# Attention with clipped Q, K, V on one core: the attention stage's queues rearranged, normalising moved from VectorE to GpSimd

## The reference

```python
xn = _layernorm(x, axis=-1)
# attention, 32 heads of 32 features
qkv = jnp.clip(jnp.einsum('bsd,ed->bse', xn, Wqkv), -8.0, 8.0)
q, k, v = jnp.split(qkv, 3, axis=-1)
q = _layer_norm(q, q_ln_w, q_ln_b); k = _layer_norm(k, k_ln_w, k_ln_b)
scores = jnp.einsum('bqhd,bkhd->bhqk', q, k) * scale + slopes * rel   # causal mask
out = jnp.einsum('bhqk,bkhd->bqhd', softmax(scores), v)
x = x + jnp.einsum('bsd,ed->bse', out, Wout) + ffn(xn, W_binarized, bias)
```

## Time and profile before

| | us |
|---|---|
| median of 3 runs | 1588.84 (1585.44 to 1590.82) |
| the profiled execution | 1590.43, span 1588.6 |
| attention, first exponential to first output product | 727.4 to 1416.7 |
| output stage, from there to the end | 1416.7 to 1588.6 |

### The profile page before, as it was taken

How to read it: one execution, slowest core, us unless ns; L and a number is a source line. 1 busy time by engine, 2 the same in 40 slices (tenths; PEclk the granted TensorE clock), 3 DMA queues, 4 the chain that set the end, 5 groups by cost and what they waited for, 6 DMA issues and landing times.

```text
span 1588.6 us, 24448 instructions
## 1 busy us (share of the span) xinstructions
PE 1430.5 (90%) x9256; PEld 661.4 (42%) x9256; DVE 835.1 (53%) x1310; ACT 558.9 (35%) x1049; POOL 549.5 (35%) x316
## 2 busy tenths in 40 slices
PE   4899999999999979998888888887978888889998
PEld 2455445445545434444333333333333333334443
DVE  6665354545454301266767677666666677631111
ACT  4444133323333200004554555454554555540000
POOL 4221122222222100001544555543345555565443
PEclk9999999999999989999999999999999999999999
DMA  6453232322222372211222222212222220025543
GB/s 232 154 166 112 67 78 60 79 60 69 70 73 66 90 204 80 77 57 42 69 69 64 67 69 56 52 46 63 70 69 64 67 69 24 20 82 166 159 146 119
DMA packets 145396, 136.85 MB, mean 86 GB/s; under 512 B 83744, under 2 KB 112416, under 8 KB 145120
## 3 DMA queue, kind: packets, MB, share of 16 engines
q1 hardware_dynamic: 48285, 90.80, 18.4%
q10 hardware_dynamic: 97027, 44.89, 12.0%
HBM read 93.06 MB, written 42.47 MB: 85 GB/s over the span
## 4 chain that ended last, share of the span: by engine, by line
PE 64%; issue 10%; DVE 10%; ACT 4%; DMA 4%; ACTq 3%; POOL 3%; SPq 2%; POOLq 0%; DVEq 0%
PE ps L956 39%; PE ps L1115 8%; PE ps L1031 5%; DVE arena L836 5%; PE ps L1092 5%; DVE arena L892 3%; ACT arena L672 3%; PE ps L1118 3%; PE ps L1009 2%; PE ps L1095 1%; PE ps L1034 1%; ACTq L335 1%; DMA arena<-r_scr 1%; ACTq L336 1%; DMA v_scr<-arena 1%
## 5 line engine op out<-in xcount | busy, mean ns | idle before, releaser
L956 PE MATMUL ps<-arena 128*128 128x512 f16 x3584 | 795.5, 382 | 21.6 <-DVE arena L807 11.3
L956 PEld LDWEIGHTS ps<-arena 128*128 128x128 f16 (+1 forms) x3584 | 349.8, 98 | 439.3 <-issue 13.7
L556 POOL TENSOR_TENSOR arena<-arena 128x2048 f32<-128x2048 f32 (+1 forms) x96 | 338.4, 3525 | 551.3 <-ACT arena L672 542.0
L836 DVE TENSOR_REDUCE arena<-ps 128x1 f16<-128x512 f32 (+3 forms) x768 | 382.3, 548 | 213.9 <-PE ps L1034 121.1
L672 ACT ACTIVATE arena<-ps 128x512 f32<-128x512 f32 (+3 forms) x768 | 326.9, 499 | 294.8 <-PE ps L1095 182.8
L1031 PE MATMUL ps<-arena 127*128 127x512 f16 (+3 forms) x768 | 249.4, 346 | 57.9 <-DVE arena L836 55.7
L1092 PE MATMUL ps<-arena 128*128 128x512 f16 (+3 forms) x768 | 253.0, 343 | 49.4 <-ACT arena L672 46.7
L807 DVE TENSOR_SCALAR arena<-ps 128x1024 f32<-128x1024 f32 x48 | 58.8, 1224 | 253.8 <-PE ps L956 225.0
L1115 PE MATMUL ps<-arena 128*32 128x512 f32 (+3 forms) x1536 | 163.4, 522 | 0.0
L1092 PEld LDWEIGHTS ps<-arena 128*128 128x128 f16 x768 | 77.0, 101 | 169.0 <-ACT arena L672 75.6
L1031 PEld LDWEIGHTS ps<-arena 127*128 127x128 f16 x768 | 76.9, 101 | 135.9 <-DVE arena L836 99.6
(11 more groups left out here) (50 smaller groups left out, 843.5 us busy)
## 6 DMA issues: line engine op xcount, KB each, us to landing
arena<-in_x SPq DMA_DIRECT2D x32, 512.0 KB, 4.6
arena<-in_wqkv_t SPq DMA_DIRECT2D x48, 256.0 KB, 4.0
base_scr<-arena SPq DMA_DIRECT2D x16, 512.0 KB, 2.9
q_scr<-arena ACTq DMA_DIRECT2D x16, 512.0 KB, 4.1
k_scr<-arena ACTq DMA_DIRECT2D x16, 512.0 KB, 4.4
v_scr<-arena SPq DMA_DIRECT2D x16, 512.0 KB, 2.9
arena<-r_scr SPq DMA_DIRECT2D x128, 64.0 KB, 2.0
arena<-base_scr SPq DMA_DIRECT2D x16, 512.0 KB, 3.8
```

The lines of the kernel that those rows point to most:

```text
L556: nc.gpsimd.tensor_tensor(acc[:, :, at:HALF], before, p32[k % PSLOTS][:, :, 0:w], ALU.add)\
L836: ins = nc.vector.tensor_reduce(negm[s % 2][:, at:at + 1], ps[:, NATB[use(s, pos) % RB], col:col + width], AX, ALU.max, negate=True)
L956: ins = nc.tensor.matmul(dst[c], lhs(k, a), wparts[:, k, b, c * HALF:(c + 1) * HALF], start=(k == 0 and (a, b) == order[0]), stop=(k == KT ...
```

## The change

The work is the same; its places change.

- The natural-score items of the next group are spread over the chunks by a table, `NATS`, and the V products get places by a table, `PV_AFTER`.
- `load_stack` and `load_vg` move from ACT's queue to SP's, behind the sums of the former group, two groups ahead in place of three.
- `o_norm` and `o_low` move from DVE to GpSimd, between the additions; in the output stage they stand ahead of the residual additions.
- O and S are copied with two ACT instructions, each with a semaphore of its own; `o_high` of the first half stands behind the exponential (0, 3) of the next group, that of the second half behind (8, 1).
- ACT and DVE no longer wait for the storing of V before attention starts; the first writers of `ot` do.

```diff
@@ -286,9 +287,17 @@
             at = max(0, P * t - HALF * qb)
             return qb, t, at, HALF - at
 
-        WORK = [span(c)[3] for c in range(NC) for j in range(GH)]
-        DUE = [ITEMS * sum(WORK[:x + 1]) // sum(WORK) for x in range(len(WORK))]
-        LAG = 2
+        NATS = [4, 3, 3, 2, 5, 4, 4, 4, 5, 4, 2, 2]
+        assert sum(NATS) == ITEMS
+
+        PV_AFTER = {(1, 0): [-2], (2, 0): [-1], (2, 3): [0], (4, 2): [1], (5, 2): [2], (6, 2): [3],
+                    (7, 1): [4], (8, 1): [5], (8, 3): [6], (10, 0): [7, 8], (11, 2): [9]}
+
+        def due(c, j):
+
+            return sum(NATS[:c]) + NATS[c] * (j + 1) // GH
+
 
 
         DIRECT = [qb == 0 or t == 0 for qb, t in CHUNKS]
@@ -413,7 +422,7 @@
 
             def sums_out(m):
 
-                sp.wait_ge(os_out, m + 1)
+                sp.wait_ge(s_out, m + 1)
                 sp.dma_start(s_scr[m], os_sb[m % 2][0:P:DH, 1, :]).then_inc(s_st, 16)
                 sp.wait_ge(s_st, 16 * (m + 1))
                 need(sp, rec_done, m - 1)
@@ -466,6 +475,14 @@
                 row_b_in(n)
                 if n > 0:
                     sums_out(blk_no(n - 1, 1))
+                    if n == 1:
+                        for s in range(2):
+                            sp.wait_ge(v_st[s], stored(NT // 2))
+                    if n < GROUPS - 1:
+                        load_vg(sp, n + 1)
+                    if n + 2 < GROUPS:
+                        sp.wait_ge(st_done, NC * GH * n)
+                        load_stack(sp, n + 2)
                 if n < GROUPS - 1:
                     row_a_in(n + 1)
                 if n > 0:
@@ -542,19 +559,51 @@
                 tile_loop(pool, qk_step)
 
 
+            def o_norm(n, qb):
+
+                m = blk_no(n, qb)
+                pool.wait_ge(r_ld, 16 * GH * (m + 1))
+                o = os_sb[m % 2][:, 0, :]
+                nc.gpsimd.tensor_tensor(o, o, rb[m % 2], ALU.mult).then_inc(on_done, 1)
+
+            def o_low(n, qb):
+
+                m = blk_no(n, qb)
+                pool.wait_ge(oh_done, m + 1)
+                if (n, qb) == (0, 0):
+                    for s in range(2):
+                        pool.wait_ge(v_st[s], stored(NT // 2))
+                part = [ot[n][:, s, qb * HALF:(qb + 1) * HALF] for s in range(2)]
+                nc.gpsimd.tensor_tensor(part[1], os_sb[m % 2][:, 0, :], part[0], ALU.subtract).then_inc(ol_done, 1)
+
+            def add_in(n, c):
+
+                qb, t, at, w = span(c)
+                k = n * NC + c
+                pool.wait_ge(exp_done, GH * (k + 1))
+                if t == 2:
+                    need(pool, pv_done, n * NC)
+                need(pool, add_done, adds_for(k) - 1)
+                former = p32[(k - 1) % PSLOTS] if t == 2 else acc[:, :, at:HALF]
+                nc.gpsimd.tensor_tensor(acc[:, :, at:HALF], former, p32[k % PSLOTS][:, :, 0:w], ALU.add)\
+                  .then_inc(add_done, 1)
+
             for n in range(GROUPS):
                 for c in range(NC):
-                    qb, t, at, w = span(c)
-                    k = n * NC + c
-                    if DIRECT[c] or t == 1:
-                        continue
-                    pool.wait_ge(exp_done, GH * (k + 1))
-                    if t == 2:
-                        need(pool, pv_done, n * NC)
-                    need(pool, add_done, adds_for(k) - 1)
-                    before = p32[(k - 1) % PSLOTS] if t == 2 else acc[:, :, at:HALF]
-                    nc.gpsimd.tensor_tensor(acc[:, :, at:HALF], before, p32[k % PSLOTS][:, :, 0:w], ALU.add)\
-                      .then_inc(add_done, 1)
+                    if not DIRECT[c] and CHUNKS[c][1] > 1:
+                        add_in(n, c)
+                    if n > 0:
+                        if c == 0:
+                            o_norm(n - 1, 0)
+                        if c == 2:
+                            o_low(n - 1, 0)
+                        if c == 6:
+                            o_norm(n - 1, 1)
+                        if c == 9:
+                            o_low(n - 1, 1)
+            for qb in range(2):
+                o_norm(GROUPS - 1, qb)
+                o_low(GROUPS - 1, qb)
 
             pool.wait_ge(bias_ld, 16)
             for t in range(NT):
@@ -677,34 +726,35 @@
                 m = blk_no(n, qb)
                 act.wait_ge(pv_done, n * NC + QB_END[qb] + 1)
                 need(act, ol_done, m - 1)
-                nc.scalar.activation(os_sb[m % 2], ps[:, O_BANK:O_BANK + 2, :], ACT.Copy).then_inc(os_out, 1)
+                nc.scalar.activation(os_sb[m % 2][:, 0, :], ps[:, O_BANK, :], ACT.Copy).then_inc(o_out, 1)
+                nc.scalar.activation(os_sb[m % 2][:, 1, :], ps[:, S_BANK, :], ACT.Copy).then_inc(s_out, 1)
 
             def o_high(n, qb):
 
                 m = blk_no(n, qb)
                 act.wait_ge(on_done, m + 1)
+                if (n, qb) == (0, 0):
+                    for s in range(2):
+                        act.wait_ge(v_st[s], stored(NT // 2))
                 nc.scalar.activation(ot[n][:, 0, qb * HALF:(qb + 1) * HALF], os_sb[m % 2][:, 0, :], ACT.Copy)\
                   .then_inc(oh_done, 1)
 
             act.wait_ge(mm_done, NT * 4)
             act.wait_ge(w_lo, ready(NT * 4 - 1))
-            for s in range(2):
-                act.wait_ge(v_st[s], stored(NT // 2))
             for n in range(GROUPS):
                 for c in range(NC):
                     for j in range(GH):
                         exps(n, c, j)
-                        if (c, j) == (2, 1) and n > 0:
-                            os_copy(n - 1, 1)
-                            if n < GROUPS - 1:
-                                load_vg(act, n + 1)
-                        if (c, j) == (7, 1) and n > 0:
-                            o_high(n - 1, 1)
-                        if (c, j) == (6, 1):
+                        if n > 0:
+                            if (c, j) == (0, 3):
+                                o_high(n - 1, 0)
+                            if (c, j) == (2, 0):
+                                os_copy(n - 1, 1)
+                            if (c, j) == (8, 1):
+                                o_high(n - 1, 1)
+                        if (c, j) == (6, 2):
                             os_copy(n, 0)
-                if n < GROUPS - STACKS:
-                    load_stack(act, n + STACKS)
-                o_high(n, 0)
+            o_high(GROUPS - 1, 0)
             os_copy(GROUPS - 1, 1)
             o_high(GROUPS - 1, 1)
 
@@ -877,40 +927,16 @@
                 need(dve, r_st, 16 * (m - 1))
                 nc.vector.reciprocal(rout[m % 2], rin[m % 2]).then_inc(rec_done, 1)
 
-            def o_norm(n, qb):
-
-                m = blk_no(n, qb)
-                dve.wait_ge(r_ld, 16 * GH * (m + 1))
-                o = os_sb[m % 2][:, 0, :]
-                nc.vector.tensor_tensor(o, o, rb[m % 2], ALU.mult).then_inc(on_done, 1)
-
-            def o_low(n, qb):
-
-                m = blk_no(n, qb)
-                dve.wait_ge(oh_done, m + 1)
-                part = [ot[n][:, s, qb * HALF:(qb + 1) * HALF] for s in range(2)]
-                nc.vector.tensor_tensor(part[1], os_sb[m % 2][:, 0, :], part[0], ALU.subtract).then_inc(ol_done, 1)
-
-            dve.wait_ge(v_st[1], stored(NT // 2))
             for n in range(GROUPS):
                 for pos in range(ITEMS):
                     if n < GROUPS - 1:
                         nat_item(n + 1, pos)
                     elif pos == 0:
                         row_out(n, use(GROUPS, 0), row_b, rowb_ld)
-                    if n > 0:
-                        if pos == 4:
-                            o_low(n - 1, 0)
-                        if pos == 16:
-                            recips(n - 1, 1)
-                        if pos == 23:
-                            o_norm(n - 1, 1)
-                        if pos == 30:
-                            o_low(n - 1, 1)
+                    if pos == 16 and n > 0:
+                        recips(n - 1, 1)
                     if pos == 31:
                         recips(n, 0)
-                    if pos == 38:
-                        o_norm(n, 0)
 
             def c_out_step(t, p):
                 dve.wait_ge(c_done, t + 1)
@@ -919,11 +945,8 @@
                 nc.vector.scalar_tensor_tensor(outc[p], banks(4 + 2 * p, 2), 1.0 / (SX * SW), basec[p],
                                                ALU.mult, ALU.add).then_inc(c_out, 1)
 
-            o_low(GROUPS - 1, 0)
+            recips(GROUPS - 1, 1)
             c_out_step(0, 0)
-            recips(GROUPS - 1, 1)
-            o_norm(GROUPS - 1, 1)
-            o_low(GROUPS - 1, 1)
             for t in range(1, NT):
                 c_out_step(t, t % 2)
 
...
@@ -1104,7 +1127,7 @@
                 p, v = p32[k % PSLOTS], vg[n % 2]
                 pe.wait_ge(exp_done, GH * (k + 1))
                 if first:
-                    need(pe, os_out, blk_no(n, qb))
+                    need(pe, o_out, blk_no(n, qb))
```

(19 more changed lines are left out.)

## The result

The changed kernel took 1596.61 us in the median of 8 runs (1594.12 to 1600.18), the kernel before 1589.44 (8 runs beside them): a ratio of 1.005, 95% interval 1.0035 to 1.0065. It is slower by half a per cent, 7 us, where 26 had been forecast. The profiled execution has a span of 1593.8 us against 1588.6, 5.2 more.

What follows compares the result with a forecast made beforehand. GpSimd's queue, through ScalarE's wait for o_norm, was taken to bound the changed kernel's groups. Groups +18.0, head -3.3, tail +11 gave +25.7 on 1590.43, 1616.1; that execution is 1.6 above the median, so 1615, range 1580 to 1645.

Steps and rivals of the forecast that it cites:

- The bound that it named: Attention groups: GpSimd's queue ends last; ScalarE waits 8 us for o_norm at o_high, TensorE some 7.
- The tail: Output stage: o_norm and o_low ahead of tile 0's additions stop TensorE 8.6 us before product 2; with slow clock +11.
- The loads: Eight loads on SP's queue ahead of the reciprocals: counted at nothing, with cover of 1 us only.
- The larger stops of before: TensorE's stops of 3.36 us for VectorE and 3.00 for ScalarE: removing them buys nothing in the groups.
- S: Rest of a group's ring, from exponential (1', 0) to the next first addition: 19.3 us, bounds 16.6 and 21.
- the slow clock: TensorE at half speed behind its stop of 7 us in each group: 1.8 us, taken into 19.3.
- All groups: Attention, first addition of group 0 to group 15: 385.6 + 15 S = 675.1 us against 657.1, +18.0.
- GpSimd's chain: Each group, first addition to exponential (1', 0): 26.0 us with o_high and handovers, of which six additions 21.15.
- a sign: Trace after the change: the group's period would be 45 to 46 us.
- The head: Before attention: ScalarE's first exponential no longer waits for the storing of V, worth -3.3 us.

Runs made afterwards that it cites:

- e2: Changed kernel with ScalarE's o_high of the first half behind exponential (3, 3) of the next group instead of (0, 3); 1548.1 us, ratio 0.974.
- e1: Changed kernel with GpSimd's o_norm and o_low of the very last half behind the residual additions of tiles 0 and 1, c_out earlier; 1588.3 us.
- e12: Changed kernel with the loads on SP's queue issued at the end of a group, behind the reciprocals of both halves; 1597.0 us, ratio 1.0038.
- e7: Changed kernel with o_norm and o_low back on VectorE and the output stage's additions ahead as before the change; 1556.4 us, ratio 0.9777.
- e4: Kernel before with only load_stack and load_vg moved to SP's queue, behind the sums of the former group; 1608.0 us, ratio 1.0095.
- e10: Kernel before with the loads on SP's queue at the end of a group, behind the reciprocals of both halves; 1565.7 us, ratio 0.9828.

## Why the prediction was wrong in size

**What held.** The bound that it named: ScalarE stands behind `o_norm` 7.5 us in each group (8 forecast), TensorE 7.4 (7). Taking that one wait away (e2) gave 48 us. The tail: a stop of 8.54 us against 8.6, +10.3 with the clock against +11, mended by e1. The loads: hidden with a cover of next to nothing (e12), and in one group not wholly. The larger stops of before bought nothing in the changed kernel.

**Luck.** S was 19.21 us against 19.3, but not by its parts. The forecast had 17.5 for the work and 1.8 for the slow clock; the length and mean clock of S give 16.7 and 2.5, as an estimate. The 16.7 is next to the forecast's lower bound of 16.6, in which all small stops close. Two errors of 0.7 to 0.8 us, each worth 11 us over fifteen groups, cancelled.

**The step that failed** is the term "All groups", 385.6 + 15 S = 675.1, +18.0, measured 657.4, +0.3. The mechanism was right and its links were mis-sized. Of the 17.7 us, 11.8 are in GpSimd's chain with `o_high`, put at 26.0 us and measured at 25.12 in a middle group (the wait of 0.74 us took a little back). The parts: the six additions take 330.6 / 16 = 20.66 us instead of 21.15. By forms, before and after:

```profile
L556 POOL TENSOR_TENSOR arena<-arena 128x2048 f32<-128x2048 f32 x36 | 167.8, 4661 | 268.9 <-ACT arena L672 265.5
...
L588 POOL TENSOR_TENSOR arena<-arena 128x2048 f32<-128x2048 f32 x38 | 172.6, 4543 | 230.6 <-ACT arena L721 228.9
...
L567 POOL TENSOR_TENSOR arena<-arena 128x512 f32<-128x512 f32 x25 | 31.6, 1265 | 0.7 <-DMA arena<-r_scr 0.7
...
L577 POOL TENSOR_TENSOR arena<-arena 128x512 f16<-128x512 f32 x24 | 27.7, 1154 | 8.9 <-ACT arena L739 8.9
```

The largest take 4.54 us instead of 4.66, since VectorE's two-input operations no longer fall between them (4.61 in e7, where they are back). `o_low` takes 0.11 less than the 1.264 put in; `o_norm` was as taken. From the end of `o_norm` to the exponential 0.56 us pass, where 0.8 had been put in for `o_high` and a handover, and 0.06 was rounding up. Together 0.9.

The other 5.9 us are in S: 17.2 us in group 0, 2.1 less than taken; 1.1 less at the last; and 19.09 in the mean of the thirteen between, 0.2 less, which makes 2.7. So the period was 44.28 and not the 45 to 46 that the prediction had named as a sign. A sum that is multiplied by fifteen must be exact to 0.1 us in each link. That the groups came out at +0.3, level with the kernel before, has no cause of its own: 25.12 + 19.1 happens to be what its periods were. The range's lower end held the result; what failed was the size, 26 us of loss against 7.

The head was -4.7 us instead of -3.3. The first exponential came 3.6 earlier; the rest is a stop of TensorE of 2.5 us behind it and a stretch at 0.50, both there before the change and neither after. That stretch isn't in every execution: e4 and e10 keep the stop, show 1.00 there, and need 159.2 and 159.9 us where the kernel before needed 161.9.

**Where the gain of the change went.** Loads on SP: in the change's place they cost against the kernel before, because they delay the reciprocals (e4, e10); in the changed kernel GpSimd hides that (e12). Norms on GpSimd: they relieve VectorE of 6 us and end its stops, but lengthen a chain that ScalarE was now made to wait for (e2, e7). Residual additions: delayed by the same operations (e1).

## What to carry to other kernels

When work moves to an idle engine, follow its queue to the next place where somebody waits for its last operation: GpSimd was 39% busy over the span, yet 25 us of its queue stood in a row, and one wait at the wrong place in ScalarE's queue cost more than all the removed stops gave. Try another place for the wait before moving the work back: `o_high` behind (3, 3) instead of (0, 3) was worth 3%. Small transfers on the critical path must not be stored behind big loads in the same queue. And in a loop, multiply the error of each link by the number of turns before trusting a sign.

## What was not expected of the hardware

- An 8 KB store took 6.1 us to land behind 2.1 MB of loads in the same queue, and 1.4 us without. The Trainium skill ("DMA: Bandwidth & Descriptors", Queues, rings and completion order) has descriptors of one ring taken in order on each DMA engine; these two times agree with it.
- VectorE and GpSimd on two SBUF inputs each: VectorE pays nearly all. Its 128x512 `o_low` took 3.60 us beside an addition and 0.68 with GpSimd idle, one group later:

```profile
1126.85 0.68 DVE L892 TENSOR_TENSOR arena<-arena 128x512 f16<-128x512 f32 x1
```

  GpSimd's 2048-wide addition took 4.66 us in the mean with such operations of VectorE about, and 4.54 without.
- GpSimd's subtraction of an f16 input with an f16 output took 1.154 us against 1.265 for the f32 multiplication of the same size; the prediction had allowed for such a difference and not used it. The Trainium skill ("GPSIMD Engine Reference", Instruction dispatch) gives some 2.5 cycles an element as a floor, an estimate of 1.07 us for 512 elements. Both rows lie above it, and by it the forecast would have been 9 us lower and still too high.
